# A patch attention and a windowed transformer on one core: the first tile's projection in halves inside the patch steps, another GpSimd order, three loads on ScalarE's queue

## The chip, the cores and the metric

One core of one Trainium2 chip runs the whole program in one launch. The metric is the device time of that core in microseconds, as the median of several runs.

## The reference

The input x has 2048 tokens of 128 numbers. It is normalized per token (`xn = layernorm(x)`), and two branches are added to it: `x + attn(xn) + ffn(xn)`.

`attn` projects xn to q, k and v for 16 heads of 8 (weights `Wqkv`, 384x128). The tokens are taken in patches of 20 with stride 2: a block of 40 tokens gives two patches, its even and its odd tokens. There are 13 blocks (520 tokens). Each patch attends within itself (softmax over 20), the results replace xn in those 520 places, and `Wout` with a bias is applied to all 2048 tokens.

`ffn` has two layers. Each shifts half of the channels by one token, projects to q, k, v (8 heads of 64, `wqkv` 128x1536), divides q and k by their norm per head, scales them, rotates them with position tables that also carry a decay (cosine and sine, for q and k), attends in windows of 64 with one window behind, and projects back with a residual. Then shift, layernorm, a gated feed-forward of 341 with exact gelu, and a second residual.

## The kernel before, in words

The five engines run programs of their own, written out by hand, with semaphores between them. "PE" is TensorE, "SP" the sync engine. The program has a first part (input normalization and patch attention) and then, for each layer, a loop over 16 tiles of 128 tokens (`over_tiles`), in which every engine works on neighbouring tiles at once.

**Input.** SP loads x in four groups of 512 tokens (L434), then the head scales (L438), `wqkv` of layer 0 (L439, into `x1_shift`, which is free in the first part), the tables `cos_w` and `sin_w` (1 MB each, L440 and L441) and the masks (L442, 576 KB). ScalarE's queue loads the small constants and the patch weights (L1070, L1071). VectorE computes the statistics (L1324, L1327), ScalarE the reciprocal deviation (logarithm L1078, exponential L1081), VectorE normalizes groups 0 and 1 (L1399), GpSimd groups 2 and 3 (L570). PE turns each group to channels by tokens (`turn_input`, L695), ScalarE copies it to `xin` (`take_input`, L1086), and SP shifts it into `xs` (L447, L449), from which ScalarE rounds `h_hi` (`round_first`, L1100) and GpSimd subtracts to `h_lo` (`split_first`, L606). A projection in fp32 accuracy is three matmuls on such high and low parts (`matmul3`, L166 to L168), and `wqkv` is rounded and split likewise (`round_part` L1103 on ScalarE, `split_wqkv` L592 on GpSimd).

**Patches.** The 13 blocks are done in seven steps of two blocks, `over_patches` with t from -1 to 7 (`A_STEPS` is 7). In step t PE does the scores of t (L743), turns the probabilities of t-1 (L753), projects the values of t (L728, from copies of `xin` that GpSimd repeats in three parts with `repeat_patches`, L563) and weighs the values of t-1 (L765). VectorE does maxima and differences of t (L1341, L1344), normalizes the output of t-2 (L1351, L1353) and masks the values of t (L1333). ScalarE copies the turned probabilities of t-1 (L1125) and makes the exponentials of t (L1129). Patch q and k come from two projections of 272 columns (`project_patch_qk`, L720 and L721) into banks 0, 1 and 6, 7; `take_patch_qk` (L1115, L1118) scales q and masks k per head. Between these, ScalarE rounds `wqkv` (steps 0 and 1), takes input groups 2 and 3 (steps 2 and 3), rounds the spans (steps 2 to 5), copies the masks (4) and rounds the feed-forward weights (6, L1147).

**GpSimd's order.** First patch repeat, groups 2 and 3 normalized, second and third repeat, cosine table times head scale (`scale_table`, L585), split of `wqkv`, sine table, splits of the four spans.

**Tile 0 of layer 0.** Behind patch step 6 PE projects q and k of tile 0 in one go to banks 0 and 1 (`project_qk`). VectorE multiplies with cosine and sine (`rotate`, L1384), ScalarE squares (`norms`, L1153), VectorE sums per head (`sum_squares`, L1374), ScalarE makes the reciprocal norms (L1157, L1160), GpSimd adds the two products (`sum_rotated`, L641) and scales (`scale_rotated`, L649). PE turns the result (L844), ScalarE copies it, and the scores start (L859, L865). Projection, rotation and the rest of tile 1 follow in the same way, with the last patch outputs turned and put away between them (`turn_patch_out` L776, `put_patches` L1362). From here the loop over the tiles runs.

Of the kernel before, what the change touches and what calls it, by code (L numbers as in the profile page):

```python
# [51 lines left out]
A_COLS = 2 * A_CHUNK  # L52
A_VAL = 36
# [122 lines left out]
def build(nc, x, a_wqkv_t, a_wout_t, wqkv, q_scale, k_scale, wo, w1, w2, vectors_d,  # L176
          cos_d, sin_d, small_d, masks_d, out):
    ctx = ExitStack()
    with ctx:
# [130 lines left out]
        a_qk_ps = [(bank(0), bank(1)), (bank(6), bank(7))]  # L310
# [35 lines left out]
        xn_late = sem("xn_late")  # L346
        xn_tr = sem("xn_tr")
# [80 lines left out]

        block = ctx.enter_context(nc.Block())

        @block.sync
        def _(sp):
# [102 lines left out]
        def _(pool):  # L535
# [37 lines left out]
            pool.wait_ge(xin0_done, 1)  # L573
            repeat_patches(0)
            normalize_input(2)
# [38 lines left out]

            pool.wait_ge(scale_in, 32)
# [17 lines left out]
            def sum_rotated(n):  # L633

                after(pool, rot_done, 2 * n + 2)
                for part in range(2):
                    after(pool, qkt_ready, 2 * n + (part - 1))
                    span = slice(part * INNER, (part + 1) * INNER)
                    to, first, second = (b[:, span].rearrange("p (h s d) -> p h s d", h=HEADS, s=2)
                                         for b in (qkn, rot1, rot2))  # L640
                    pool.tensor_tensor(to, first, second[:, :, ::-1, :], ALU.add).then_inc(rot_summed, 1)  # L641
# [45 lines left out]
        def _(pe):  # L687
# [27 lines left out]

            def project_patch_qk(chunk):
                span = slice(1 + chunk * A_CHUNK, 1 + (chunk + 1) * A_CHUNK)
                pe.wait_ge(xin0_done, chunk + 1)
                q_ps, k_ps = a_qk_ps[chunk]
                pe.matmul(q_ps[:, 0:A_CHUNK], a_wqkv_s[:, 0:DIM], xin[:, span], start=True, stop=True)  # L720
                pe.matmul(k_ps[:, 0:A_CHUNK], a_wqkv_s[:, DIM:2 * DIM], xin[:, span],  # L721
                          start=True, stop=True).then_inc(a_qk_done, 1)
# [14 lines left out]
            def patch_scores(t):  # L737
                after(pe, a_qk_taken, 2 if t * A_STEP + A_STEP + 24 > A_CHUNK else 1)
# [18 lines left out]
            def weigh_patch_values(t):  # L757
                after(pe, a_pt_done, t + 1)
                after(pe, a_v_done, t + 1)
                after(pe, a_o_done, t)  # L760
                if t == 0:
                    pe.wait_ge(a_qk_taken, 2)
# [62 lines left out]
            turn_patch_out(0)  # L825
            project_qk(0, 1)
# [241 lines left out]
        def _(act):  # L1068

            act.dma_start(small[:], small_d).then_inc(const_in, 16)  # L1070
            act.dma_start(a_wqkv_s[:], a_wqkv_t).then_inc(aw_in, 16)  # L1071
            act.preload_act_table_set("natural_log_exp_and_others")
# [38 lines left out]
            def take_patch_qk(chunk):  # L1111
                act.wait_ge(a_qk_done, chunk + 1)
                span = slice(chunk * A_CHUNK, (chunk + 1) * A_CHUNK)
                q_ps, k_ps = a_qk_ps[chunk]
                act.mul(a_q[:, span], q_ps[:, 0:A_CHUNK], A_SCALE)  # L1115

                for h in range(4):
                    k = act.mul(a_k[:, h, span], k_ps[:, 0:A_CHUNK], head_mask[:, h:h + 1])  # L1118
                k.then_inc(a_qk_taken, 1)

            def patch_step(t, parity):
# [9 lines left out]
                if t == 0:  # L1131
                    take_patch_qk(1)
                if t in (2, 3):
                    take_input(t)
                if t in (0, 1):
                    if t == 0:
                        act.wait_ge(wqkv_in[0], 16)
                    round_part(0, t * W_PART)
                if t in (2, 3, 4, 5):
                    round_first(t - 2)  # L1140
                if t == 4:
                    act.wait_ge(masks_in, 16)
                    act.copy(masks[:], masks_f).then_inc(masks_done, 1)
                if t == 6:
                    act.wait_ge(w1_in, 16)
# [28 lines left out]
            norms(0)  # L1174
            inverse_norms(0)
# [144 lines left out]
        def _(dve):  # L1320
# [43 lines left out]
            def patch_step(t, parity):  # L1364
                if there(t, A_STEPS):
                    patch_differences(t)
                if there(t - 2, A_STEPS):
                    patch_out(t - 2)
                if there(t, A_STEPS):
                    patch_values(t)  # L1370

            def sum_squares(n):
                after(dve, sq_done, n + 1)
                dve.reduce_sum(ss, sq[:].rearrange("p (h d) -> p h d", d=DH), AX.X).then_inc(ss_done, 1)  # L1374
                after(dve, ss_done, 2 * n + 1)
                after(dve, lnss_done, n)
                dve.tensor_reduce(ssc[:], ss_pair[:], AX.X, ALU.max).then_inc(ss_done, 1)  # L1377

# [272 lines left out]
```

## Time and profile before

| what | us |
|---|---|
| median of 3 runs | 379.59 (376.76 to 379.63) |
| the profiled execution | 379.34 |
| its span, from the first to the last instruction | 377.5 |
| PE, ScalarE, VectorE, GpSimd busy in the span | 344.2, 285.3, 268.9, 250.5 |

The profile is of one execution. A row of the timeline gives the start, the length, the engine, the line, what is written from what, the number of merged instructions, and in brackets how long the engine stood idle before and what ended that. "issue" is idle time in which the engine waited for nothing that the profile shows. The mean granted clock of TensorE over the span is 0.991 of full speed.

### The profile page before, as it was taken

Reading aid. Unit: us, or ns where it says so; the run is one execution under the profiler, and the core shown is the slowest. Engines: PE = TensorE matmul, PEld = TensorE weight load, DVE = VectorE, ACT = ScalarE, POOL = GpSimd, SP = SyncE. Lnnn points to the kernel's source line nnn. Section 1 sums busy time; section 2 is a strip of 40 time slices with the busy share of each in tenths; the row PEclk is TensorE's granted clock in tenths of the full one; section 3 lists DMA queues with packets and bytes.
Section 4 is the critical chain, followed back from the end, with each engine's and each line's share of the span. In section 5 each row is a group of like instructions: output and inputs, shape, how many; then the busy total and the mean of one; then the engine's idle time right before and its main releaser. Section 6 shows DMA issues by size and latency. Waiting matters only on the chain. (4 is left out here: it accounts for less than half of the span.)

```text
span 377.5 us, 10808 instructions
## 1 busy us (share of the span) xinstructions
PE 344.2 (91%) x4015; PEld 264.3 (70%) x4015; DVE 268.9 (71%) x474; ACT 285.3 (76%) x881; POOL 250.5 (66%) x242
## 2 busy tenths in 40 slices
PE   1758779999999999998998989999999999999996
PEld 0557557888888888667565667778888887666565
DVE  4636677878887888657868767878887887565544
ACT  2746378998999899888635689989899989886321
POOL 2999479999989999821015778788989898320000
PEclk9999899999999999999999999999999999999999
DMA  6986032222232222270020322232223222200011
GB/s 201 372 158 184 5 126 56 65 68 55 65 71 66 51 64 65 65 259 16 9 56 0 71 69 67 52 76 58 56 61 79 58 65 61 55 7 16 20 36 56
DMA packets 35954, 28.68 MB, mean 76 GB/s; under 512 B 19221, under 2 KB 29375, under 8 KB 35391
## 3 DMA queue, kind: packets, MB, share of 16 engines
q1 hardware_dynamic: 35615, 27.54, 27.8%
q8 instruction: 32, 0.52, 0.6%
q10 hardware_dynamic: 288, 0.46, 0.4%
q14 instruction: 19, 0.16, 0.1%
HBM read 9.64 MB, written 1.05 MB: 28 GB/s over the span
## 5 line engine op out<-in xcount | busy, mean ns | idle before, releaser
L1204 ACT ACTIVATE probs<-ps,neg_max 128x128 f32<-128x128 f32 x256 | 90.1, 376 | 6.2 <-DVE neg_max L1438 5.4
L641 POOL TENSOR_TENSOR qkn<-work 128x512 f32<-128x512 f32 x64 | 80.6, 1281 | 12.3 <-DVE work L1384 9.2
L655 POOL TENSOR_TENSOR probs_n<-probs,row_inv 128x512 f32<-128x512 f32 x64 | 66.9, 1045 | 21.8 <-DVE row_inv L1443 19.9
L649 POOL TENSOR_TENSOR qkn<-qkn,rnorm 128x512 f32<-128x512 f32 x64 | 65.6, 1046 | 17.0 <-ACT rnorm L1160 16.5
L1204 ACT ACTIVATION_READ_ACCUMULATOR probs<-ps,neg_max 128x1 f32 x256 | 55.1, 215 | 0.0
L1153 ACT ACTIVATE work<-ps 128x1024 f32<-128x1024 f32 x32 | 32.8, 1026 | 18.2 <-issue 12.3
L1374 DVE TENSOR_REDUCE ss_pair<-work 128x16 f32<-128x1024 f32 x32 | 39.0, 1220 | 8.2 <-ACT work L1153 6.2
L166 PE MATMUL ps<-wqkv_hi,h_hi 128*128 128x512 f32 x96 | 42.5, 442 | 1.6 <-ACT work L1153 1.6
L1438 DVE TENSOR_REDUCE neg_max<-ps 128x4 f32<-128x512 f32 x64 | 41.0, 682 | 3.3 <-PE ps L865 3.3
L1384 DVE TENSOR_TENSOR work<-ps,cos_w 128x1024 f32<-128x1024 f32 x32 | 38.7, 1210 | 2.3 <-PE ps L168 2.3
L1384 DVE TENSOR_TENSOR work<-ps,sin_w 128x1024 f32<-128x1024 f32 x32 | 38.7, 1210 | 0.0
L879 PE MATMUL ps<-small,probs_n 128*128 128x128 f32 x256 | 36.7, 281 | 2.0 <-ACT q_t L1186 1.4
L168 PE MATMUL ps<-wqkv_hi,h_lo 128*128 128x512 f32 x96 | 38.4, 400 | 0.0
L167 PE MATMUL ps<-wqkv_lo,h_hi 128*128 128x512 f32 x96 | 38.3, 399 | 0.0
L844 PE MATMUL ps<-small,qkn 128*128 128x128 f32 x256 | 35.9, 276 | 2.5 <-POOL qkn L649 2.5
L905 PE MATMUL ps<-o_t,wo_s 128*128 128x128 f32 x256 | 36.7, 286 | 1.4 <-ACT o_t L1217 1.4
L844 PEld LDWEIGHTS ps<-small,qkn 128*128 128x128 f32 x256 | 29.2, 141 | 11.3 <-issue 3.3
L905 PEld LDWEIGHTS ps<-o_t,wo_s 128*128 128x128 f32 x256 | 31.3, 191 | 8.0 <-issue 6.4
L865 PE MATMUL ps<-k_t,q_t 64*64 64x128 f32 x1024 | 33.4, 269 | 0.0
L1443 DVE RECIPROCAL row_inv<-row_sum 128x4 f32<-128x4 f32 x64 | 11.4, 178 | 30.7 <-ACT probs L1204 28.1
L896 PE MATMUL ps<-probs_t,v_off 128*64 128x64 f32 x512 | 33.1, 228 | 0.0
L1449 DVE COPY probs_t<-ps 128x512 f32<-128x512 f32 x32 | 22.1, 692 | 15.3 <-PE ps L879 15.3
(156 smaller groups left out, 731.3 us busy)
## 6 DMA issues: line engine op xcount, KB each, us to landing
v_off<-v_tok SPq DMA_DIRECT2D x64, 128.0 KB, 2.3
k_t<-k_t SPq DMA_DIRECT2D x30, 128.0 KB, 2.3
cos_w<-in_cos_t SPq DMA_DIRECT2D x2, 1024.0 KB, 7.8
sin_w<-in_sin_t SPq DMA_DIRECT2D x2, 1024.0 KB, 10.7
x<-xin SPq DMA_DIRECT2D x16, 128.0 KB, 2.4
x_shift<-x SPq DMA_DIRECT2D x64, 32.0 KB, 1.8
x_raw<-in_x SPq DMA_DIRECT2D x4, 256.0 KB, 4.6
x_shift<-in_wqkv SPq DMA_DIRECT2D x1, 768.0 KB, 8.6
```

What stands on the lines that cost most here:

```text
L166: pe.matmul(out, s_hi, m_hi, start=start, stop=False)
L167: pe.matmul(out, s_hi, m_lo, start=False, stop=False)
L168: return pe.matmul(out, s_lo, m_hi, start=False, stop=stop)
L641: pool.tensor_tensor(to, first, second[:, :, ::-1, :], ALU.add).then_inc(rot_summed, 1)
L649: pool.tensor_tensor(of, of, rnorm[:, part * HEADS:(part + 1) * HEADS].unsqueeze(2) .broadcast_to([P, HEADS, DH]), ALU.mult).then_inc(rot_ ...
L655: pool.tensor_tensor(probs_n[:, 4 * g:4 * g + 4, :], probs[:, 4 * g:4 * g + 4, :], row_inv[:, 4 * g:4 * g + 4].unsqueeze(2).broadcast_to([ ...
L844: mm = pe.transpose(turn_ps[:, at:at + P], qkn[:, at:at + P], ident)
L905: mm = pe.matmul(y_ps[:, 0:P], wo_s[:, layer, c, :], o_t[:, c * P:(c + 1) * P], start=(c == 0), stop=(c == CHUNKS - 1))
L1204: e = act.activation(probs[:, k, :], s_ps[g][:, cw * P:(cw + 1) * P], ACT.Exp, bias=neg_max[:, k:k + 1], accum_out=row_sum[:, k:k + 1])
L1374: dve.reduce_sum(ss, sq[:].rearrange("p (h d) -> p h d", d=DH), AX.X).then_inc(ss_done, 1)
L1384: dve.tensor_tensor(to[:].rearrange("p (a h d) -> p a h d", a=2, d=DH), qk_ps.rearrange("p (a h d) -> p a h d", a=2, d=DH), table[:, t, :, ...
L1438: dve.tensor_reduce(neg_max[:, 4 * g:4 * g + 4], s_ps[g].rearrange("p (c k) -> p c k", c=4), AX.X, ALU.max, negate=True).then_inc(max_done, 1)
```

## The change

Six things are done together, all in the first part.

1. The loads of `cos_w`, `sin_w` and the masks are issued on ScalarE's queue, behind the constants, instead of SP's.
2. GpSimd's order becomes: first repeat, group 2 normalized, cosine table, split of `wqkv`, split of span 0, second and third repeat, group 3 normalized, sine table, splits of spans 1 to 3.
3. ScalarE rounds both halves of `wqkv` and span 0 in step 0, takes the second part of patch q and k in step 1 (before: step 0), rounds span 1 in step 2, copies the masks in step 3, takes group 3 and rounds span 2 in step 4 (PE turns group 3 there too), rounds span 3 in step 6, and rounds the feed-forward weights behind the reciprocal norms of tile 0.
4. The parts of patch q and k are of 280 and 264 (q) and 280 and 240 (k) columns, and the second part shares bank 6, so that bank 7 is free.
5. Tile 0 is projected in halves, q in patch step 5 and k in step 6, into bank 6. VectorE rotates them in steps 6 and 7, ScalarE squares them there; products and squares go to `x1_shift` and `x_patch`, which are free then. The second half waits for the first half's square. The row sums and reciprocal norms of tile 0 stand in step 7.
6. Behind the patches only tile 1 is projected.

```diff
+A_Q_CHUNKS = [(0, 280), (280, A_COLS - 280)]
+A_K_CHUNKS = [(0, 280), (280, PATCHED - 280)]
...
-        a_qk_ps = [(bank(0), bank(1)), (bank(6), bank(7))]
+        a_qk_ps = [(bank(0), bank(1)), (bank(6), bank(6)[:, A_Q_CHUNKS[1][1]:])]
+        first_ps = bank(6)
...
+        def rot_of(n):
+            if isinstance(n, int) and n == 0:
+                return x1_shift[:, 1:1 + 2 * INNER], x1_shift[:, 1 + 2 * INNER:1 + 4 * INNER]
+            return rot1, rot2
+        def sq_of(n):
+            return x_patch[:, 0:2 * INNER] if isinstance(n, int) and n == 0 else sq
...
-            sp.dma_start(cos_w[:], cos_d).then_inc(cos_in, 16)
-            sp.dma_start(sin_w[:], sin_d).then_inc(sin_in, 16)
-            sp.dma_start(masks_f, masks_d).then_inc(masks_in, 16)
...
-            normalize_input(3)
-            pool.wait_ge(xin0_done, 2)
-            repeat_patches(1)
-            repeat_patches(2)
...
             scale_table(cos_w, cos_in)
             split_wqkv()
+            split_first(0)
+            pool.wait_ge(xin0_done, 2)
+            repeat_patches(1)
+            repeat_patches(2)
+            normalize_input(3)
             scale_table(sin_w, sin_in)
-            for g in range(SPANS):
+            for g in range(1, SPANS):
                 split_first(g)
...
+            def project_first(part):
+                if part == 0:
+                    pe.wait_ge(h_split, 1)
+                    pe.wait_ge(wqkv_split, 1)
+                    pe.wait_ge(xin0_done, SPANS)
+                else:
+                    pe.wait_ge(first_q_squared, 1)
+                span = slice(part * INNER, (part + 1) * INNER)
+                matmul3(pe, first_ps, input_tile(0), (wqkv_hi[:, 0, span], wqkv_lo[:, 0, span])).then_inc(
+                    qk_ready if part else first_q_ready, 1)
...
-                if t in (2, 3):
+                if t in (2, 4):
...
-                    turn_input(t)
+                    turn_input(2 if t == 2 else 3)
...
+                if t in (5, 6):
+                    project_first(t - 5)
...
-                if t == A_STEPS:
-                    pe.wait_ge(wqkv_split, 1)
-                    pe.wait_ge(a_dif_done, A_STEPS)
-                    project_qk(0, 0)
...
+            act.dma_start(cos_w[:], cos_d).then_inc(cos_in, 16)
+            act.dma_start(sin_w[:], sin_d).then_inc(sin_in, 16)
+            act.dma_start(masks_f, masks_d).then_inc(masks_in, 16)
             act.preload_act_table_set("natural_log_exp_and_others")
...
                 if t == 0:
+                    act.wait_ge(wqkv_in[0], 16)
+                    for part in range(W_PARTS):
+                        round_part(0, part * W_PART)
+                    round_first(0)
+                if t == 1:
                     take_patch_qk(1)
...
+                if t in (6, 7):
+                    square_first(t - 6)
+                if t == A_STEPS:
+                    inverse_norms(0)
                     act.wait_ge(w1_in, 16)
...
+            def square_first(part):
+                act.wait_ge(rot_done if part else first_q_rotated, 2)
+                act.activation(sq_of(0)[:, part * INNER:(part + 1) * INNER], first_ps, ACT.Square).then_inc(
+                    sq_done if part else first_q_squared, 1)
...
+                if t in (6, 7):
+                    if t == 6:
+                        dve.wait_ge(wqkv_split, 1)
+                        dve.wait_ge(tables_done, 4)
+                    rotate_first(t - 6)
                 if there(t, A_STEPS):
                     patch_values(t)
+                if t == A_STEPS:
+                    sum_squares(0)
...
+            def rotate_first(part):
+                dve.wait_ge(qk_ready if part else first_q_ready, 1)
+                for table, to in zip((cos_w, sin_w), rot_of(0)):
+                    dve.tensor_tensor(to[:, part * INNER:(part + 1) * INNER].rearrange("p (h d) -> p h d", d=DH),
...
             over_patches(dve, patch_step, in_front)
-            dve.wait_ge(tables_done, 4)
-            rotate(0, 0, cos_w)
-            rotate(0, 0, sin_w)
             patch_out(A_STEPS - 1)
-            sum_squares(0)
+            rotate(1, 1, cos_w)
             put_patches(0)
-            rotate(1, 1, cos_w)
             rotate(1, 1, sin_w)
```

## Rows read from the trace of the kernel before

**Rows 1.** The page's first line.

```profile
span 377.5 us, 10808 instructions
```

**Rows 2.** Timeline, 38 to 50 us: start, length, engine, line, tiles, count.

```profile
38.31 0.50 PE L166 MATMUL ps<-wqkv_hi,h_hi 128*128 128x512 f32 x1
...
40.08 1.23 DVE L1384 TENSOR_TENSOR work<-ps,cos_w 128x1024 f32<-128x1024 f32 x1 [1.05 <-PE ps L168]
...
42.53 1.02 ACT L1153 ACTIVATE work<-ps 128x1024 f32<-128x1024 f32 x1 [1.50 <-DVE work L1384]
42.60 2.51 POOL L641 TENSOR_TENSOR qkn<-work 128x512 f32<-128x512 f32 x2 [5.50 <-DVE work L1384]
...
43.58 1.22 DVE L1374 TENSOR_REDUCE ss_pair<-work 128x16 f32<-128x1024 f32 x1 [0.66 <-ACT work L1153]
...
43.70 0.76 PE L166 MATMUL ps<-wqkv_hi,h_hi 128*128 128x512 f32 x1 [1.58 <-ACT work L1153]
...
45.69 2.05 POOL L649 TENSOR_TENSOR qkn<-qkn,rnorm 128x512 f32<-128x512 f32 x2 [0.58 <-ACT rnorm L1160]
...
46.63 1.23 DVE L1384 TENSOR_TENSOR work<-ps,cos_w 128x1024 f32<-128x1024 f32 x1 [1.21 <-PE ps L168]
...
47.72 1.03 PE L844 MATMUL ps<-small,qkn 128*128 128x128 f32 x8
...
49.48 0.41 PE L859 MATMUL ps<-masks 64*64 64x512 bf16 x4 [0.73 <-ACT k_t L1193]
```

**Rows 3.** Timeline, 26 to 36 us: patch steps 3 to 6.

```profile
26.15 0.42 PE L743 MATMUL ps<-work 32*32 32x80 f32 x26 [3.53 <-issue]
...
28.22 1.88 PE L728 MATMUL ps<-a_wqkv_s,qkn 128*80 128x128 f32 x8
...
33.11 0.44 PE L743 MATMUL ps<-work 32*32 32x80 f32 x32
...
34.94 0.29 DVE L1353 TENSOR_TENSOR x_patch<-ps,a_inv 128x128 f32<-128x128 f32 x1
...
35.78 0.37 PE L743 MATMUL ps<-work 32*32 32x80 f32 x16
```

**Rows 4.** DMA queues from 23.4 to 23.6 us: packets, MB, share of 16 engines.

```profile
q1 hardware_dynamic: 104, 0.05, 112.4%
q8 instruction: 1, 0.02, 38.3%
```

**Rows 5.** Timeline, 10 to 28 us: GpSimd.

```profile
10.74 3.19 POOL L570 TENSOR_SCALAR xn_tok<-x_raw,mv,rstd 128x128 f32<-128x128 f32 x4
...
17.67 1.22 POOL L563 COPY qkn<-xin 128x480 f32<-128x480 f32 x2
...
19.25 4.67 POOL L585 TENSOR_TENSOR cos_w<-cos_w,qk_scale 128x1024 f32<-128x1024 f32 x2
...
23.89 3.42 POOL L592 TENSOR_TENSOR wqkv_lo<-x_shift,wqkv_hi 128x1536 fp32r<-128x1536 f32 x1
```

**Rows 6.** Timeline, 16 to 19 us: ScalarE.

```profile
16.36 1.62 ACT L1118 ACTIVATE work<-ps,small 128x272 f32<-128x272 f32 x4
...
17.84 0.86 ACT L1103 CAST wqkv_hi<-x_shift 128x768 fp32r<-128x768 f32 x1
```

**Rows 7.** Timeline from 5 us; stretch 10 to 15 us (GB/s last); queues 3 to 5 us.

```profile
5.56 2.08 SPq L441 DMA_DIRECT2D sin_w<-in_sin_t  x1
...
5.80 0.30 ACT L1078 ACTIVATE ln<-mv,eps_s 128x4 f32<-128x4 f32 x1 [2.84 <-DVE mv L1327]
...
8.46 0.84 DVE L1324 BATCH_NORM_STATS2 stats<-x_raw 128x6 f32<-128x128 f32 x4
...
10.00:15.00 5.00, 3.85 (x49) 2.63 (x48) 2.98 (x14) 2.99 (x9) 4.26 (x7) 1.00 1.02 425
...
q1 hardware_dynamic: 921, 0.46, 76.7%
q10 hardware_dynamic: 174, 0.23, 31.5%
```

More of the change, by code:

```diff
@@ L346, in build @@
         xn_late = sem("xn_late")
+        first_q_ready = sem("first_q_ready")
+        first_q_rotated = sem("first_q_rotated")
+        first_q_squared = sem("first_q_squared")
         xn_tr = sem("xn_tr")
@@ L613, in split_w1 @@
                                    ALU.subtract).then_inc(w1_split, 1)
+            pool.wait_ge(xin0_done, 1)
+            repeat_patches(0)
+            normalize_input(2)
             pool.wait_ge(scale_in, 32)
@@ L635, in sum_rotated @@
                 after(pool, rot_done, 2 * n + 2)
+                if isinstance(n, int) and n == 0:
+                    pool.wait_ge(a_vr_done, A_STEPS)
                 for part in range(2):
@@ L639, in sum_rotated @@
                     to, first, second = (b[:, span].rearrange("p (h s d) -> p h s d", h=HEADS, s=2)
-                                         for b in (qkn, rot1, rot2))
+                                         for b in (qkn, *rot_of(n)))
                     pool.tensor_tensor(to, first, second[:, :, ::-1, :], ALU.add).then_inc(rot_summed, 1)
@@ L714, in project_qk @@
                 mm.then_inc(qk_ready, 1)
+            def project_first(part):
[8 more added lines that the diff above has]
+                    qk_ready if part else first_q_ready, 1)
             def project_patch_qk(chunk):
-                span = slice(1 + chunk * A_CHUNK, 1 + (chunk + 1) * A_CHUNK)
                 pe.wait_ge(xin0_done, chunk + 1)
                 q_ps, k_ps = a_qk_ps[chunk]
-                pe.matmul(q_ps[:, 0:A_CHUNK], a_wqkv_s[:, 0:DIM], xin[:, span], start=True, stop=True)
-                pe.matmul(k_ps[:, 0:A_CHUNK], a_wqkv_s[:, DIM:2 * DIM], xin[:, span],
+                (q_at, q_size), (k_at, k_size) = A_Q_CHUNKS[chunk], A_K_CHUNKS[chunk]
+                pe.matmul(q_ps[:, 0:q_size], a_wqkv_s[:, 0:DIM], xin[:, 1 + q_at:1 + q_at + q_size],
+                          start=True, stop=True)
+                pe.matmul(k_ps[:, 0:k_size], a_wqkv_s[:, DIM:2 * DIM], xin[:, 1 + k_at:1 + k_at + k_size],
                           start=True, stop=True).then_inc(a_qk_done, 1)
@@ L737, in patch_scores @@
             def patch_scores(t):
-                after(pe, a_qk_taken, 2 if t * A_STEP + A_STEP + 24 > A_CHUNK else 1)
+                after(pe, a_qk_taken, 2 if t * A_STEP + A_STEP + 24 > A_K_CHUNKS[0][1] else 1)
                 after(pe, a_dif_done, t)
@@ L825, in _ @@
             turn_patch_out(0)
+            pe.wait_ge(a_dif_done, A_STEPS)
             project_qk(0, 1)
@@ L1112, in take_patch_qk @@
                 act.wait_ge(a_qk_done, chunk + 1)
-                span = slice(chunk * A_CHUNK, (chunk + 1) * A_CHUNK)
                 q_ps, k_ps = a_qk_ps[chunk]
-                act.mul(a_q[:, span], q_ps[:, 0:A_CHUNK], A_SCALE)
+                (q_at, q_size), (k_at, k_size) = A_Q_CHUNKS[chunk], A_K_CHUNKS[chunk]
+                act.mul(a_q[:, q_at:q_at + q_size], q_ps[:, 0:q_size], A_SCALE)
                 for h in range(4):
-                    k = act.mul(a_k[:, h, span], k_ps[:, 0:A_CHUNK], head_mask[:, h:h + 1])
+                    k = act.mul(a_k[:, h, k_at:k_at + k_size], k_ps[:, 0:k_size], head_mask[:, h:h + 1])
                 k.then_inc(a_qk_taken, 1)
@@ L1131, in patch_step @@
                 if t == 0:
-                    take_patch_qk(1)
[L1133 to L1141, printed above, removed]
+                    act.wait_ge(wqkv_in[0], 16)
[3 more added lines that the diff above has]
+                if t == 1:
+                    take_patch_qk(1)
+                if t == 2:
+                    take_input(2)
+                    round_first(1)
+                if t == 3:
                     act.wait_ge(masks_in, 16)
                     act.copy(masks[:], masks_f).then_inc(masks_done, 1)
+                if t == 4:
+                    take_input(3)
+                    round_first(2)
                 if t == 6:
+                    round_first(3)
+                if t in (6, 7):
+                    square_first(t - 6)
+                if t == A_STEPS:
+                    inverse_norms(0)
                     act.wait_ge(w1_in, 16)
@@ L1173, in _ @@
             over_patches(act, patch_step, in_front)
-            norms(0)
-            inverse_norms(0)
             for layer in range(LAYERS):
@@ L1368, in patch_step @@
                     patch_out(t - 2)
+                if t in (6, 7):
[3 more added lines that the diff above has]
+                    rotate_first(t - 6)
                 if there(t, A_STEPS):
                     patch_values(t)
+                if t == A_STEPS:
+                    sum_squares(0)
             def sum_squares(n):
                 after(dve, sq_done, n + 1)
-                dve.reduce_sum(ss, sq[:].rearrange("p (h d) -> p h d", d=DH), AX.X).then_inc(ss_done, 1)
+                dve.reduce_sum(ss, sq_of(n).rearrange("p (h d) -> p h d", d=DH), AX.X).then_inc(ss_done, 1)
                 after(dve, ss_done, 2 * n + 1)
@@ L1377, in sum_squares @@
                 dve.tensor_reduce(ssc[:], ss_pair[:], AX.X, ALU.max).then_inc(ss_done, 1)
+            def rotate_first(part):
+                dve.wait_ge(qk_ready if part else first_q_ready, 1)
+                for table, to in zip((cos_w, sin_w), rot_of(0)):
+                    dve.tensor_tensor(to[:, part * INNER:(part + 1) * INNER].rearrange("p (h d) -> p h d", d=DH),
+                                      first_ps.rearrange("p (h d) -> p h d", d=DH),
+                                      table[:, 0, part, :].unsqueeze(1).broadcast_to([P, HEADS, DH]),
+                                      ALU.mult).then_inc(rot_done if part else first_q_rotated, 1)
             def rotate(n, t, table):
```

5 lines of the change are left out of this document (removed).

## The prediction

> **What bounds the kernel now.** I read the page first: a span of 377.5 us [rows 1] in an execution of 379.34, so 1.84 us lie around the span. The measured runs have a median of 379.59, 0.25 above the profiled execution, so a sum made against 379.34 can be set beside the median directly. The diff touches nothing behind the first tiles of layer 0, and the rest of the program is a chain that repeats the same step; whatever the first part wins, the rest starts earlier by it. So the question is when the first tile's scores start, now 49.48 us [rows 2].
>
> The timeline from 38 to 50 us gives the end of the first part; read it from the bottom. The scores (L859) follow ScalarE's copies of the turned q and k, those the turns (L844, 47.72), those GpSimd's scaling (L649, 45.69 for 2.05), which began 2.11 us after VectorE's row sums (L1374, 43.58). Ahead of these ScalarE's squares (L1153) waited for VectorE's two rotations (L1384, the first at 40.08), and these for the projection of tile 0, which began at 38.31, 1.77 us ahead of the first rotation. GpSimd's sum (L641, 42.60) starts beside the squares. All this stands behind the last patch steps, one link after another, with PE idle in between: 1.58 us ahead of the row at 43.70 [rows 2].
>
> The timeline of PE from 26 to 36 us shows the other loss. 26 of the 32 score matmuls of patch step 3 run at 26.15, behind 3.53 us of "issue", a gap in the middle of one row of matmuls with nothing waited for. Behind it the clock is at its lower level (1.2 GHz): the values' group at 28.22 takes 1.88 us for what should be about 1.0. Steps 5 and 6 start at 33.11 and 35.78, 2.67 apart [rows 3]. The DMA view of a slice inside the gap has a 16 KB packet of instructions among 104 of kernel data [rows 4]. I read the gap as a block of PE's program that came late through full DMA engines. That is inferred: the trace names no releaser.
>
> The Trainium skill (Runtime: NRT & Kernel Launch, Instruction fetch mechanics) says that programs are refilled in blocks of 256 instructions over a DMA queue of the sequencer's own, and the packet of [rows 4] agrees; it also gives PE room for 2048 instructions. By that size nothing could be missing this early, the gap would have another cause and would stay, which is the time of the rival "the gap stays".
>
> **GpSimd's new order.** The first normalization (10.74, 3.19) ends at 13.93. The cosine table takes 4.67 and now follows at once, if it has landed: 18.6. The weight split takes 3.42: 22.0; it needs both rounded halves. ScalarE makes them one after the other behind its exponentials of step 0, where the taking of patch q and k stood (from 16.0), at 0.86 each [rows 6]: 17.8, in time. Splitting the first span, 512 columns by the 3.42 for 1536, with a little overhead 1.25: 23.3. The second patch repeat 1.22: 24.5, the third under 0.5: 24.9. The last normalization, as the first, 3.19: 28.1. The sine table, as the cosine's, 4.67: 32.8 [rows 5]. So the patches now wait for GpSimd twice: 24.5 (values of step 3) and 28.1 (turning input span 3).
>
> **The patch steps.** ScalarE's taking of the second part of patch q and k, 1.62 for k [rows 6] and 0.4 for q, moves behind the roundings and ends at 21.2. PE waits for it ahead of turning input span 2, about 0.7 us later than before, and step 3 starts near 23.0. That costs nothing, for the values of step 3 wait for GpSimd until 24.5; without this cover it costs 0.7. The new sizes (280 and 264 or 240 columns for twice 272) change a 0.4 us instruction by a few hundredths: 0. Step 3's values and weighing, about 1.5 at the upper clock, bring step 4 to 26.0; its scores and turn end at 26.9, and PE stands until 28.1 for the normalized span. From there turning the input, values and weighing, about 2.0, bring step 5 to 30.1 against 33.11 [rows 3]: 3.0 us. Here I count the unexplained gap as gone, since tables and masks travel beside x from the start instead of behind it, all traffic ends earlier, and up to 2 us of a gap disappear in the two waits. Bounds of this term: 3.0, and 0 if the gap stays.
>
> **The projection in halves.** Step 6 starts a step and half a projection after 30.1: 2.67 + 0.8 gives 33.5. VectorE's normalized output ends 2.12 us after a step's scores start (34.94 + 0.29 against 33.11) [rows 3]: 35.6. It now adds the first two half rotations, at half of 1.23 and a little, 0.65 each: 36.9. The square is 1.02 for a whole, so 0.6: 37.5. PE has stood since about 35.3 by then, 2 us; the idle 1.58 of [rows 2] was followed by the lower clock, where the projection needed 2.93 us until its rotation (43.70 to 46.63) against 1.77. A half is then 1.5, not 0.9: 39.0. The second half's rotations: 40.3, and GpSimd's sum starts there, against 42.60. Second square: 40.95. From the row sums to the scaling 2.11: 43.05; the sum's 2.51 ends at 42.8, in time. Scaling 2.05: 45.1, against 47.74: 2.6 us [rows 2]. The turn of q can start at half of this, while before all eight turns came together at 47.72; that is worth 0 to 0.6. Rounding the feed-forward weights (twice 682 columns, under 1.7 by the 0.86 for 768 [rows 6]) moves behind the norms, from 43 on, where ScalarE has nothing else until the turn of q: 0, or 0.5 if that comes sooner. The second tile's projection waits for the second square and the last patch turns: about 42 instead of 43.7, so its sum keeps in step.
>
> Sum: 2.6 + 0.4 = 3.0 us at the lower clock, 3.9 if the clock stays up. I take 3.0, because the nearest row fell: 379.34 - 3.0 = 376.3.
>
> **The queue change.** Three issues move from SP to ScalarE, ahead of its table load and its first logarithm. The sine table's issue alone took 2.08 us on SP; with two short ones it is about 3, against 2.84 us in which ScalarE stood ahead of that logarithm [rows 7]. Price 0 to 0.3; I take 0. For SP nothing waited on them but the shifted copies of the input, whose data no longer stand behind 2.6 MB on one queue.
>
> **Rivals.** *The gap stays* (some 3.5 us inside step 3). For: the DMA engines carry the same bytes at that time of the program. Then step 3's scores end at 26.2 to 26.9, at the low clock; turn and values (1.1 and 1.9) follow, step 5 starts at 32.4 to 33.8, and 3.0 becomes 0.7 to nothing: 378.6 to 379.5, middle 378.8. Against: the traffic ends earlier, and 2 us are covered.
>
> *x comes late* (the other side). Two queues share 16 engines. In 3 to 5 us, beside the constants, x's queue had 76.7% of the time and the other 31.5%, 0.46 against 0.23 MB [rows 7]; 0.57 MB of x is then left. By an even share it takes some 1.0 us more, and VectorE's statistics of the third group, at 8.46 behind its own work and not behind a transfer [rows 7], hide it. If the tables' large pieces go first, 2.6 MB at 425 GB/s [rows 7] are 6.2 us, the statistics stand for them, and with 1 us of that hidden all the rest moves 5.2: 376.3 + 5.2 = 381.5, slower than before from 4.1 us of such lateness on. If only 1.5 us come through, on GpSimd's normalization at 10.74 and so on both waits for GpSimd, it is 377.8. Against it stands the measured share.
> The Trainium skill (DMA: Bandwidth & Descriptors, Queues, rings and completion order) says that each engine changes between queues only after a packet of some 9 to 17 descriptors. With 8 KB pieces of a table against 512 B pieces of x that would be this rival at nearly its full price. The share in [rows 7] is of pieces of one to two KB and can't decide it.
>
> *Better than forecast*: clock up and gap gone, 375.4.
>
> **How the numbers follow.** Forecast 0.48; gap stays 0.28; x partly late 0.10; x late 0.06; better 0.08. The forecast's own range is 375.2 to 377.4; 8 in 10 over all cases is 374.5 to 379.6. About 1% (3.8 us) is what a measurement of this kernel can tell from no change; that line is 375.8. A third of the forecast's cases, nearly all of the better ones and some of what I have not seen lie below it: faster 0.34, within 1% 0.58, slower by over 1% 0.08.
>
> **What would show it.** Right: no "issue" gap of over 1 us in step 3; values of step 3 released by GpSimd's repeat near 24.5; step 5 near 30; GpSimd's sum of tile 0 near 40.3; scores near 46.4. Wrong: a gap of 3 us there; statistics of x released by DMA behind 9 us; the first logarithm behind 6.1; the first scores behind 48.

## The result and the profile after

The changed kernel is slower: 382.47 us as the median of 4 runs (381.65 to 384.15), ratio to before 1.0122, 95% interval 1.0076 to 1.0169. Forecast were 376.3 us, with 374.5 to 379.6 as the range. Before had 379.13 in the 4 runs beside it; over the 35 runs that all comparisons gave it, its median is 377.65, so the execution profiled before (379.34) was one of its longer ones. (One of the 35 took 946.71 us at a mean clock of 0.377 of full speed; the ratios leave it out.) The ratios here and in the table below come from the single runs of both kernels and are not quotients of the medians: 382.47 over 379.13 is 1.0088, and over 377.65 it is 1.0128.

The profile page of the changed kernel, its first line, answers [rows 1]. The busy times are those of before within 3 us (PE 347.1 against 344.2); the 3.8 us more of span are waiting and a slower clock.

```profile
span 381.3 us, 10810 instructions
```

The timeline of the start, where [rows 7] stood: start, length, engine, line, and in brackets the idle time ahead and its releaser.

```profile
3.79 4.04 SPq L454 DMA_DIRECT2D qk_scale<-in_k_scale  x1
...
13.64 0.87 DVE L1362 BATCH_NORM_STATS2 stats<-x_raw 128x6 f32<-128x128 f32 x4 [5.22 <-DMA x_raw<-in_x]
```

VectorE stands 5.22 us for the third group of x, whose statistics start at 13.64 instead of 8.46. GpSimd's normalization moves from 10.74 to 15.46, and PE's first patch scores from 13.64 to 17.24. Even SP's issues stand: that of the key scale takes 4.04 us (0.47 before), so the weights' load is issued at 7.86 (4.36 before). The DMA queues of 5 to 12 us (packets, MB, share of 16 engines) say why. q10 is ScalarE's queue with the tables, q1 is SP's with x:

```profile
q10 hardware_dynamic: 417, 2.66, 91.5%
q1 hardware_dynamic: 489, 0.24, 11.5%
```

In seven microseconds the tables moved 2.66 MB and everything on x's queue 0.24 MB. The share of 76.7 to 31.5 in favour of x's queue [rows 7], on which the forecast leaned, turned round as soon as the pieces of the second queue were large. The counts show how: the same view from 6 to 10 us has 208 packets and 1.57 MB of the tables' queue against 209 packets and 0.11 MB of x's. A packet of this view is one piece, so the two queues got equal numbers of pieces, and the bytes went by the size of a piece, some 7.5 KB against 0.5 KB. The direction is that of the rule which the forecast took from the Trainium skill (DMA: Bandwidth & Descriptors, Queues, rings and completion order), by which an engine changes queue only after a whole packet of descriptors. Equal counts fit it; how many pieces make one turn this view does not show. The forecast named the rule and gave the case 0.06.

The patch steps, the timeline that answers [rows 3] and [rows 6]:

```profile
22.05 1.57 ACT L1130 CAST wqkv_hi<-x_shift 128x768 fp32r<-128x768 f32 x2 [2.43 <-DMA x_shift<-in_wqkv]
...
24.67 0.47 PE L791 MATMUL ps<-probs,o_t 80*32 80x36 f32 x32 [2.11 <-ACT o_t L1152]
...
26.71 1.08 PE L709 MATMUL ps<-small,xn_tok 128*128 128x128 f32 x4 [0.63 <-ACT work L1145]
...
27.59 1.92 PE L756 MATMUL ps<-a_wqkv_s,probs_t 128*80 128x128 f32 x8
```

ScalarE waits 2.43 us for the weights, and behind these roundings stands the copy that PE needs for weighing step 0 (2.11 us of idle PE). Then PE waits for the second part of patch q and k, and its clock is down (1.92 for the values' group, at a granted clock of 0.50 from 27 to 29 us). Step 3 starts at 30.07 and step 5 at 35.45. No row of step 3 is split by an "issue" gap, and neither the repeat nor the normalization of GpSimd makes PE wait.

The end of the first part, for [rows 2]:

```profile
42.88 0.50 PE L168 MATMUL ps<-wqkv_hi,h_hi 128*128 128x512 f32 x1 [1.27 <-ACT x_patch L1186]
...
45.42 2.55 POOL L655 TENSOR_TENSOR qkn<-x_shift 128x512 f32<-128x512 f32 x2 [2.56 <-DVE x_shift L1430]
...
46.62 0.78 PE L168 MATMUL ps<-wqkv_hi,h_hi 128*128 128x512 f32 x1
...
47.94 2.05 POOL L663 TENSOR_TENSOR qkn<-qkn,rnorm 128x512 f32<-128x512 f32 x2
...
51.00 1.03 PE L868 MATMUL ps<-small,qkn 128*128 128x128 f32 x8
...
52.76 0.41 PE L883 MATMUL ps<-masks 64*64 64x512 bf16 x4 [0.73 <-ACT k_t L1231]
```

GpSimd's scaling ends at 49.99, but the turns start at 51.00: PE comes too late, because tile 1's projection stands ahead of them in its order: from its start to the turns it is 4.38 us (51.00 - 46.62), most of it at the lower clock. Before, this was much the same, 4.02 us (47.72 - 43.70), also at the lower clock (0.50 from 44 to 46 us), but it ended when the scaling did. A view by stretches (last three numbers: granted clock, DMA share, GB/s) shows the clock; from 44 to 46 us it is 0.50 too:

```profile
46.00:50.00 4.00, 4.00 (x14) 3.31 (x15) 2.13 (x5) 1.83 (x4) 3.98 (x4) 0.50 0.00 0
```

The first scores start at 52.76 instead of 49.48, 3.3 us later; the other 0.5 of the span come behind them.

### The profile page after: what moved, and what is told of

Read it like the earlier page. It is cut to its first block and busy times, and to the rows that moved or that the text cites. A ratio compares the mean times of both kernels' runs of the same rounds, so it can differ in the third digit from the quotient of the medians.

```text
span 381.3 us, 10810 instructions
## 1 busy us (share of the span) xinstructions
PE 347.1 (91%) x4015; PEld 265.9 (70%) x4015; DVE 268.7 (70%) x476; ACT 285.4 (75%) x882; POOL 250.5 (66%) x242
## 3 DMA queue, kind: packets, MB, share of 16 engines
q1 hardware_dynamic: 35183, 24.86, 25.1%
## 5 line engine op out<-in xcount | busy, mean ns | idle before, releaser
L655 POOL TENSOR_TENSOR qkn<-work 128x512 f32<-128x512 f32 x62 | 78.0, 1280 | 7.9 <-DVE work L1440 4.7
L1193 ACT ACTIVATE work<-ps 128x1024 f32<-128x1024 f32 x31 | 31.8, 1027 | 17.0 <-issue 12.6
L1419 DVE TENSOR_REDUCE ss_pair<-work 128x16 f32<-128x1024 f32 x31 | 37.8, 1220 | 7.8 <-ACT work L1193 5.9
L1440 DVE TENSOR_TENSOR work<-ps,cos_w 128x1024 f32<-128x1024 f32 x31 | 37.5, 1210 | 1.8 <-PE ps L170 1.8
L1440 DVE TENSOR_TENSOR work<-ps,sin_w 128x1024 f32<-128x1024 f32 x31 | 37.5, 1210 | 0.0
```

The lines of the kernel that those rows point to most:

```text
L1193: act.activation(sq[:], qk_ps, ACT.Square).then_inc(sq_done, 1)
L1419: dve.reduce_sum(ss, sq_of(n).rearrange("p (h d) -> p h d", d=DH), AX.X).then_inc(ss_done, 1)
L1440: dve.tensor_tensor(to[:].rearrange("p (a h d) -> p a h d", a=2, d=DH), qk_ps.rearrange("p (a h d) -> p a h d", a=2, d=DH), table[:, t, :, ...
```

## The experiments

Theory A after the result: the early table loads are the loss, the rest gains as forecast. Theory B: the new orders and the halves cost too. Twelve kernels were run; the column "first scores" and the steps are PE's starts in the timelines of the profiled executions, "gap" is the longest "issue" time inside step 3. Each row of steps is one execution: differences of a few tenths between rows can be the execution's.

| run | us, median | ratio, 95% interval | step 0 | step 3 | step 5 | first scores | gap |
|---|---|---|---|---|---|---|---|
| before | 377.65 | 1 | 13.64 | 22.29 | 33.11 | 49.48 | 3.53 |
| changed | 382.47 | 1.0122 (1.0076 to 1.0169) | 17.24 | 30.07 | 35.45 | 52.76 | none |
| e1 changed, tables on SP | 382.55 | 1.0139 (1.0102 to 1.0176) | 13.60 | 27.30 | 32.83 | 50.18 | none |
| e2 before, tables early on ScalarE's | 378.78 | 1.0036 (1.0017 to 1.0054) | 16.47 | 26.59 | 32.02 | 48.04 | none |
| e3 changed, tables later | 380.19 | 1.0084 (1.0054 to 1.0115) | 13.86 | 23.77 | 32.66 | 48.70 | 1.04 |
| e4 before, small loads late | 376.12 | 0.9966 (0.9936 to 0.9997) | 13.60 | 24.18 | 29.74 | 47.94 | none |
| e5 changed, no halves | 381.39 | 1.0098 (1.0063 to 1.0133) | 17.21 | 28.12 | 34.87 | 50.89 | none |
| e9 before with halves | 378.37 | 1.0021 (0.9998 to 1.0045) | 13.84 | 23.84 | 30.50 | 47.86 | 0.95 |
| e10 before, tables later | 377.94 | 1.0005 (0.9981 to 1.0029) | 13.74 | 24.06 | 30.64 | 47.06 | 0.88 |
| e11 e10, small loads late | 376.24 | 0.9970 (0.9949 to 0.9992) | 13.44 | 24.01 | 29.57 | 45.58 | none |
| e12 both orders, tables later | 378.35 | 1.0009 (0.9985 to 1.0034) | 13.79 | 23.78 | 32.10 | 48.31 | 1.94 |
| e13 GpSimd's order, tables later | 380.21 | 1.0074 (1.0044 to 1.0104) | 13.71 | 24.03 | 33.52 | 49.53 | 1.19 |
| e14 ScalarE's order, tables later | 378.01 | 0.9989 (0.9965 to 1.0013) | 13.75 | 23.92 | 31.68 | 48.08 | 1.38 |
| e15 e11, roundings in step 1 | 376.14 | 0.9963 (0.9932 to 0.9993) | 13.58 | 23.43 | 28.83 | 45.66 | none |

"Tables later" means on ScalarE's queue behind its first reciprocal deviation, "small loads late" that wo, the patch output weights, w2 and the vectors are issued behind the last shifts of the input.

**e1.** The queue change undone in the changed kernel.

```diff
+            sp.dma_start(cos_w[:], cos_d).then_inc(cos_in, 16)
+            sp.dma_start(sin_w[:], sin_d).then_inc(sin_in, 16)
+            sp.dma_start(masks_f, masks_d).then_inc(masks_in, 16)
...
-            act.dma_start(cos_w[:], cos_d).then_inc(cos_in, 16)
-            act.dma_start(sin_w[:], sin_d).then_inc(sin_in, 16)
-            act.dma_start(masks_f, masks_d).then_inc(masks_in, 16)
```

> The changed kernel with cosine, sine and masks issued on SP's queue again, behind the weights, all else kept. Theory A (the queue change made x's third and fourth groups and the layer's weights late, the rest of the change wins as forecast): the statistics of group 3 start near 8.5 us instead of 13.6, the first scores near 46 us instead of 52.8, time 375 to 377.5. Theory B (the new order and the halves cost what is missing, the late x is mostly hidden): time 380 to 383, first scores behind 50 us though x is in time.

Theory A fell. x is in time (third group at 8.34), step 0 is at 13.60, and yet the time is as bad. The timeline of ScalarE and PE:

```profile
20.95 0.62 ACT L1127 CAST h_hi<-x 128x512 fp32r<-128x512 f32 x1 [3.52 <-DMA x<-xin]
...
22.11 0.47 PE L794 MATMUL ps<-probs,o_t 80*32 80x36 f32 x32 [3.03 <-ACT o_t L1152]
```

ScalarE's rounding of span 0 stands in step 0 now, and the shifted input that it needs lies behind 2.6 MB of tables on SP's queue. PE waits 3.03 us for the copy behind it. So the new order needs weights and shifted input early, which neither place of the table loads gives: on ScalarE's queue the weights were late (2.43), on SP's the shift (3.52). The price can be estimated: e1 is 5.2 us above the before of its series (382.55 and 377.34), and the halves, still in it, cost 0.7 to 1.8 (e9 and e3, below), so the orders with the tables on SP cost some 3.4 to 4.5 us.

**e2.** The same three lines moved to ScalarE's queue in the kernel before, nothing else.

> The kernel before with nothing changed but the three loads issued on ScalarE's queue. Theory A: the third group of x lands near 13.5 us, patch step 0 starts 3.6 us late, the time is 3.5 to 6 us above that of before, less what the issue gap of step 3 gives back if it goes (up to 3.5): 380 to 385. Theory B: within 1 us of before.

x is late here too:

```profile
12.90 0.87 DVE L1324 BATCH_NORM_STATS2 stats<-x_raw 128x6 f32<-128x128 f32 x4 [4.36 <-DMA x_raw<-in_x]
```

Step 0 moves 2.8 us, but the time only by 0.36% (1.4 us), below what A expected: the patches with the old orders wait for nothing that is late afterwards, and there is no gap in step 3, which PE reaches only at 26.59 here (more on this at e4).

**e3.** The changed kernel with the loads on the same queue, later.

```diff
-            act.dma_start(cos_w[:], cos_d).then_inc(cos_in, 16)
...
                     input_rstd(0)
+                    act.dma_start(cos_w[:], cos_d).then_inc(cos_in, 16)
+                    act.dma_start(sin_w[:], sin_d).then_inc(sin_in, 16)
+                    act.dma_start(masks_f, masks_d).then_inc(masks_in, 16)
```

> The changed kernel with the three loads still on ScalarE's queue, but issued only behind its first reciprocal deviation, near 6.2 us, when most of x is in. Theory A with large packets going first as the mechanism: x is in time (group 3 statistics near 8.5 us), only the layer's weights and first shift share with the tables; time 375 to 378. If two queues slow each other whatever their order: the weights land as late as 22 us and time stays above 379.

x is in time (8.59) and 2.3 us come back, not the 5 to 7 that A wanted. Now the waits that the forecast had foreseen stand in PE's timeline, later than foreseen, since GpSimd stands for the cosine table first:

```profile
16.69 4.69 POOL L589 TENSOR_TENSOR cos_w<-cos_w,qk_scale 128x1024 f32<-128x1024 f32 x2 [2.64 <-DMA cos_w<-in_cos_t]
...
27.31 1.07 PE L756 MATMUL ps<-a_wqkv_s,qkn 128*80 128x128 f32 x8 [1.18 <-POOL qkn L575]
...
30.83 0.63 PE L709 MATMUL ps<-small,xn_tok 128*128 128x128 f32 x4 [1.10 <-POOL xn_tok L582]
```

**e4.** The kernel before with one block of issues moved.

```diff
+            shift_input(2)
+            shift_input(3)
             sp.dma_start(wo_s[:], wo.rearrange("l (c p) n -> p l c n", p=P)).then_inc(w_in, 16)
...
-            shift_input(2)
-            shift_input(3)
```

> The kernel before with the loads of wo, a_wout, w2 and the vectors issued behind the last two shifts of the input (near 30 us) instead of at 15 us. If the 3.5 us gap in PE's step 3 is an instruction block late through full DMA engines: the gap goes or falls below 1 us and the time is 2 to 4 us below that of before. If the gap has another cause: it stays at 3.5 us at the same matmul and the time is within 0.7 us of before.

The gap in step 3 is gone, and its 32 matmuls are one row:

```profile
24.18 0.44 PE L743 MATMUL ps<-work 32*32 32x80 f32 x32
```

In time it gives 0.34%, 1.3 us, less than the 2 to 4 expected: the usual gap is nearer to 1 us than to the 3.53 of [rows 3]. Every profiled variant in which step 3 starts near 24 us with the small loads in flight has it, between 0.88 and 1.94 (e3, e9, e10, e12, e13, e14), and none with the small loads late (e4, e11, e15). In all seven profiles that have the gap, that of before included, it stands behind the sixth of the 32 matmuls and ends at about the same time, between 25.13 and 26.15 us. Its length is then mostly a matter of when PE arrives. The profiled execution of before arrived at 22.29, because its step 0 ran at nearly twice the speed (1.10 us for the values' group at 14.01, against 2.00 for the same group in e4, though the granted clock reads 1.00 in both); behind its long gap the clock was down, so that it reached step 5 at 33.11, later than e10 (30.64), whose gap was 0.88. The profiles that arrive after 26.2 us (changed, e1, e2, e5) have no gap, whatever their loads.

e4 did not remove all of it. In step 6, where the small loads and the later weights are now in flight, another gap stands in the middle of a row, and behind it the projection of tile 0 runs at the lower clock (0.50 from 36 to 38 us):

```profile
34.78 0.39 PE L728 MATMUL ps<-a_wqkv_s,work 128*80 128x128 f32 x2 [1.22 <-issue]
```

The same row has 0.68 in e10, 0.67 in e11, 1.50 in e15, 0.40 in e2 and e14, and none in before.

**e5.** The changed kernel without the halves: the projection, the rotations, the squares and the sums of tile 0 stand behind the patches as before.

```diff
-                if t in (5, 6):
-                    project_first(t - 5)
...
+                if t == A_STEPS:
+                    pe.wait_ge(wqkv_split, 1)
+                    pe.wait_ge(a_dif_done, A_STEPS)
+                    project_qk(0, 0)
```

> The changed kernel (its queue and its orders) with tile 0 projected, rotated and squared in one piece behind the patches, as before. If the halves cost time (PE waits for the first half's square with the last patch step queued behind it): from the start of step 5 to the first scores 16.0 to 16.4 us instead of 17.3, time 0.5 to 1.5 us below that of the changed kernel. If the halves gain what they were forecast to gain: 1 us or more above it.

As expected of the theory that the halves cost: 1.1 us less than the changed kernel in the median (the intervals overlap), and 16.02 us from step 5 to the first scores (50.89 - 34.87) where the halves take 17.31 (52.76 - 35.45). This stretch alone proves little: e3, with the halves, has 16.04 and e4, without them, 18.20.

**e9.** The halves alone, with the queues and orders of before (the steps of the change that belong to GpSimd's and ScalarE's order undone, the loads on SP).

> The halves alone: GpSimd's and ScalarE's order and the queues of before, tile 0 in halves, the feed-forward weights rounded behind the norms. If the halves cost time: 378 to 379 where before has 377.3, and 17.0 to 17.4 us from step 5 to the first scores. If the halves gain and only the queue and the orders cost: 375.5 to 376.8.

378.37, ratio 1.0021 with an interval down to 0.9998: no gain, at most a small loss. Step 5 to the first scores takes 17.36. PE waits for the first half's square and the rest runs at the lower clock:

```profile
38.23 0.80 PE L168 MATMUL ps<-wqkv_hi,h_hi 128*128 128x512 f32 x1 [1.27 <-ACT x_patch L1180]
...
40.00:44.00 4.00, 3.33 (x27) 2.60 (x26) 3.07 (x6) 1.69 (x5) 2.54 (x3) 0.50 0.00 0
```

**e10.** The kernel before with the later table loads of e3.

> The kernel before with the three loads on ScalarE's queue, issued behind its first reciprocal deviation. If the place of the issue is what made x late: group 3's statistics at 8.5 us, step 0 at 13.7, the shifted input in early, no long gap in step 3, time 374 to 376.5, below both before and the variant with the early issue (378.8). If the queue itself costs: 378 or more.

377.94: neither gain nor loss (1.0005). So the loads cost nothing on ScalarE's queue if they are issued later, where issued early they cost 0.36% (e2; the two intervals overlap a little). But the gain expected did not come, and a gap of 0.88 us stands in step 3.

**e11.** Both edits together, later tables and late small loads.

> As the last, with wo, a_wout, w2 and the vectors also issued behind the last shifts. If an instruction block in PE's step 3 is late through full DMA engines: no gap over 0.5 us in steps 2 to 4 and 0 to 1.5 us below the last; if the gap has nothing to do with this traffic, equal to it within 0.4 us.

No gap in step 3, 376.24, 1.7 us below e10 (expected 0 to 1.5; the two intervals overlap a little). It beats both kernels by a small amount: 0.9970, interval 0.9949 to 0.9992.

**e12, e13, e14.** The orders without the halves and with the later tables: both (e12), GpSimd's alone with group 3 turned in step 4 (e13), ScalarE's alone, also with group 3 in step 4 (e14). All three keep the new sizes of patch q and k. The edit of e13 against e12:

```diff
                 if t == 0:
-                    act.wait_ge(wqkv_in[0], 16)
-                    for part in range(W_PARTS):
-                        round_part(0, part * W_PART)
-                    round_first(0)
-                if t == 1:
                     take_patch_qk(1)
...
+                if t in (0, 1):
+                    if t == 0:
+                        act.wait_ge(wqkv_in[0], 16)
+                    round_part(0, t * W_PART)
+                if t in (2, 3, 5, 6):
+                    round_first(t - 2 if t < 4 else t - 3)
```

> Both new orders, no halves, the tables issued behind the first reciprocal deviation. Against the same with halves (380.2): if the halves cost about 1 us, 379.2 and 16.0 to 16.4 us from step 5 to the first scores. Against the old orders with the same late tables (377.9): the two orders cost 1 to 2 us. If the orders cost nothing: 378 or less.

> As the last with ScalarE's roundings and taking of patch q and k where they were before, so GpSimd's order alone (and group 3 turned in step 4). If GpSimd's order costs (it waits for the cosine table, and repeats and normalization, which the patches wait for, stand behind 12 us of tables and splits): PE waits for GpSimd in steps 3 and 4 by 2 to 4 us in sum, time 1 to 2 us above 377.9. If ScalarE's order is the costly one: within 0.5 us of 377.9.

> As the last but one with GpSimd's order of before, so ScalarE's order alone. If ScalarE's order costs (its copy for the first weighing and its taking of patch q and k stand behind roundings that wait for weights and the shifted input): step 3 starts 1 to 2 us later than at 24.1 and PE waits for ScalarE in steps 1 and 2, time 1 to 2 us above 377.9. If it is only GpSimd's: within 0.5 us.

GpSimd's order alone costs (1.0074), for GpSimd waits 2.56 us for the cosine table and 0.97 for roundings that ScalarE makes later; PE then waits for the repeat in step 3:

```profile
28.04 1.75 PE L754 MATMUL ps<-a_wqkv_s,qkn 128*80 128x128 f32 x8 [1.49 <-POOL qkn L573]
```

ScalarE's alone does not (0.9989), and both together do not either (1.0009), against the expectation of 1 to 2 us for both. So with the tables later the two orders together are neutral, and e12 beside e3 (1.0084) shows the halves' cost with intervals that don't meet: 1.8 us. e12 beside e5 (381.39), the same kernel but for the place of the table loads, shows theirs: 3.0 us, where with the old orders the same move costs 0.8 (e2 against e10). The loss thus adds up along one chain of kernels: before to e12 0.7 us in the medians (not clear of nothing), e12 to e5 3.0 for the early tables under the new orders, e5 to the changed kernel 1.1 for the halves.

Where the halves' 1.8 us lie the profiles of e3 and e12 tell: their first scores are 0.4 apart (48.70 and 48.31), and the other 1.4 come behind these. There PE's clock falls once more in e3, in the scores of tile 1; e12 has 1.00 in the same stretch:

```profile
56.00:58.00 2.00, 2.00 (x16) 1.37 (x18) 1.55 (x3) 1.55 (x3) 1.92 (x3) 0.50 0.26 65
```

Five profiles have this second fall, three with the halves (e1, e3, e9) and two without (e5, e15), so it is not the halves' alone. But the mean granted clock of every execution points the same way: 0.982 to 0.991 in e3 against 0.989 to 1.000 in e12, 0.987 to 0.991 in the changed kernel against 0.994 to 0.996 in e5, 0.985 to 0.991 in e9 (one of ten at 1.000) against 0.991 to 1.000 in e10. As far as these means show, the halves leave PE at its lower clock for longer.

**e15.** e11 with both roundings of the weights in step 1, behind its exponentials.

```diff
-                if t in (0, 1):
-                    if t == 0:
-                        act.wait_ge(wqkv_in[0], 16)
-                    round_part(0, t * W_PART)
+                if t == 1:
+                    act.wait_ge(wqkv_in[0], 16)
+                    for part in range(W_PARTS):
+                        round_part(0, part * W_PART)
```

> The best so far (tables behind the first reciprocal deviation, small loads late, old orders; 376.24) with the first rounding of the weights moved from step 0 behind the exponentials of step 1, ahead of no copy that PE waits for. If the waits of the patch steps set the time of the first part: the 1.4 us that PE waits for ScalarE in step 1 fall to about 0.5, steps start 0.8 us earlier, 375.2 to 375.8. If GpSimd's tables and splits set it: no change, 376.0 to 376.5.

Step 3 starts 0.6 earlier and step 5 0.7, but the first scores don't (45.66 against 45.58), and the time is that of e11: 376.14, 0.9963. A gap of "issue" of 1.50 us at 34.16 in its PE timeline (0.67 in e11) took the difference in the profiled execution, which also has the second fall of the clock and, at 377.52, is longer than the median; whether it does in every one was not tried.

## Why the prediction was wrong

**What bounds the kernel.** The view was right that a shift of the first scores goes through to the end: behind them the spans of before, of the changed kernel and of e2 differ by 0.5 us (328.0, 328.5 and 328.5, the span less the first scores). It isn't free of exceptions: e1, e3, e5, e9 and e15 need 329.0 to 329.7, and these are the five in which the clock falls again in the scores of tile 1; the other nine need 328.0 to 328.5.

**The gap as 3.0 us of gain.** The term was mis-sized. That an instruction block comes late through full DMA engines fits e4 and e11, where moving the small loads removes the gap of step 3. But one profiled execution had 3.53 us of it while the other profiles have about 1 us, and the median of 379.59 that stood beside it was of three runs. Step 5, which the forecast moved from 33.11 to 30.1, stands at 30.64 in e10, where only the tables' issue is changed and the gap is still there: most of the 3.0 us was the profiled execution and no gain. Taking the gap away is worth 1.3 us (e4) or 1.7 us (e11 against e10). That the changed kernel has no gap came true by luck: not because the traffic ended earlier, but because PE reached step 3 at 30.07, after the time at which the gap ends in every profile that has it. The rival by the Trainium skill (Runtime: NRT & Kernel Launch, Instruction fetch mechanics), by which PE has room for 2048 instructions and the gap must have another cause and stay, fell: it went when loads were moved (e4). That the late thing is an instruction block is still inferred; no trace names it.

**The queue change at 0.** This is the first failed step. Its rival "x comes late" named the right mechanism with too low a chance. The share of two queues was read from a stretch in which x's queue carried pieces of 0.5 KB and the other of 1.3 KB (0.46 MB in 921 packets, 0.23 MB in 174 [rows 7]; not both one to two KB, as the forecast says), and carried over to pieces of 8 KB. The lateness of the statistics came out as priced, 5.2 us (13.64 - 8.46), but not what it does: step 0 moved 3.6 us, and the time 1.4 with the old orders (e2) and 3.0 with the new ones (e5 against e12), where the rival moved all the rest by 5.2. That its 381.5 is near the 382.47 measured is luck: the orders and the halves made up for what the late x didn't cost.

**ScalarE's order at 0.** The second failed step. "17.8, in time" looked at GpSimd, who takes the result, and not at what waits for weights and shift, nor at who is queued behind those waits: the copy for the first weighing. In the changed kernel that is 2.43 us of wait and with the clock behind it steps 0 to 3 take 12.83 us instead of the forecast 9.4. Part of this is one execution's clock: e5, with the same orders and loads, takes 10.91. Up to step 5 the changed kernel takes 18.21 and e5 17.66, where e2, with the old orders and x nearly as late, takes 15.55; so some 2.1 to 2.7 us are the orders'. And the forecast's 9.4 leaned on an execution that had 8.65 up to step 3, where e10 has 10.32. With the tables later the same order costs nothing (e14, e12): it was the order together with late weights or a late shift. The 0.7 us priced for taking patch q and k later had no cover, since GpSimd was not yet what PE waited for.

**GpSimd's order.** The waits at 24.5 and 28.1 were foreseen and stand in e3, at 27.31 and 30.83; the cosine table's landing (2.64 us of wait in e3), named as a condition, was not priced. In the changed kernel other delays covered them; in e5 they stand again, with 0.41 and 1.09 us. Alone this order costs 0.74% (e13).

**The halves.** Forecast 10.2 us from step 5 to GpSimd's sum, measured 9.97; but before needed only 9.49 (42.60 - 33.11), so this part of the change never had a gain in the forecast's own numbers, and the sum of 3.0 hid that by adding it to the gap. From the sum to the first scores the forecast had 6.1, measured were 7.34. It set the turns of tile 0 by GpSimd's scaling alone (45.1) and put tile 1's projection at 42, but in PE's order that projection stands ahead of the turns, and from its start to them before had 4.02 us (43.70 to 47.72 [rows 2]): by the forecast's own rows the turns would start near 46.0. In the changed kernel these were 4.38 us, and PE came 1 us behind GpSimd. Whole, the halves cost 1.1 us (e5), 1.8 us (e3 against e12) and 0.7 us (e9, hardly clear of nothing).

What stays open: how the 2.3 us between the changed kernel and e3 divide between late x and late weights, for both move together with the table loads; the gap in step 6; and why the clock falls a second time in some executions.

## What to carry to other kernels

A second DMA queue is no free lane: before large loads are put beside a stream of small pieces that the start of the kernel waits for, measure the share of both queues with pieces of those sizes, or issue the large ones once the small ones are in. When an operation is moved up in an in-order engine, price each thing it waits for at its landing time and list what stands behind it. And a gain read from one profiled execution is to be checked against the spread of the runs, and for what set its other end, before it becomes the largest term of a sum.

## What the runs showed of the hardware

With 8 KB pieces on one queue and 512 B pieces on the other, 16 engines gave them 91.5% and 11.5% of their time over 7 us, 2.66 against 0.24 MB, and in numbers the same (208 against 209 pieces from 6 to 10 us of it); an issue of a 64 KB load on the small pieces' queue then took 4.04 us, where it took 0.47 without the other queue's tables. With a load of small pieces in flight PE stood in the middle of a group of matmuls for 0.88 to 3.53 us with nothing waited for, behind the same matmul and until 25.1 to 26.2 us in seven profiles, and moving that load away removed this gap, but one of up to 1.50 us stood in step 6 then; that it is the fetching of PE's program is inferred. In the changed kernel PE ran at its lower clock from 44 to 50 us, after idle times of 1.27 us and less between short pieces of work, and this stretched the next tile's projection (0.63 us for a row that takes 0.39 at the full clock). Before had the lower clock there too, from 44 to 46 us.
